# GRU stage: ScalarE writes the conditioning shift into the accumulation banks, fewer fill products, one VectorE operation for the early part of the state

## The reference, cut to what matters

```
h = 0
for t in range(128):
    z = sigmoid(x[t] @ Wz + h @ Uz + cond @ Cz + bz)
    r = sigmoid(x[t] @ Wr + h @ Ur + cond @ Cr + br)
    cand = tanh(x[t] @ W + (r * h) @ U + cond @ C + b)
    h = (1 - z) * h + z * cand
    out[t] = h
```

## Time and profile before

| | |
|---|---|
| time, median of 3 runs | 4519.89 us (4518.96 to 4525.05) |
| profiled execution, own time | 4519.17 us |
| span of its instructions | 4517.4 us, mean granted TensorE clock 0.969 |
| TensorE busy, whole span | 4151.1 us, 92% |
| VectorE busy | 2454.7 us, 54% |
| ScalarE busy | 1958.4 us, 43% |
| GpSimd busy | 782.6 us, 17% |

### The profile page before, as it was taken

The page is one execution under the profiler, slowest core; times in us unless marked ns, Lnnn a source line. Parts: engine busy times, 40 slices in busy tenths (PEclk is TensorE's granted clock), DMA queues, the critical chain, the costliest instruction groups (busy, mean ns, idle before and its releaser), DMA issues. The chain is left out here.

```text
span 4517.4 us, 116966 instructions
## 1 busy us (share of the span) xinstructions
PE 4151.1 (92%) x40700; PEld 2927.5 (65%) x40896; DVE 2454.7 (54%) x7214; ACT 1958.4 (43%) x4989; POOL 782.6 (17%) x3252
## 2 busy tenths in 40 slices
PE   6998999999998899998799998999998797889999
PEld 4555776778776455554355787887876455556666
DVE  5775664555554677775555344666666553431111
ACT  4333443333332666665233222666665352333333
POOL 1111221000000466664222000111111210000000
PEclk9999999999999999999799998999999898989999
DMA  1000000000000000000000000000000100000000
GB/s 55 0 0 25 1 0 26 1 0 0 0 0 10 1 2 1 1 1 1 34 0 0 4 0 0 3 3 3 3 3 2 54 0 1 0 0 3 5 5 7
DMA packets 4098, 29.01 MB, mean 6 GB/s; under 512 B 433, under 2 KB 945, under 8 KB 2353
## 3 DMA queue, kind: packets, MB, share of 16 engines
q1 hardware_dynamic: 3776, 24.97, 1.4%
HBM read 22.87 MB, written 2.10 MB: 6 GB/s over the span
## 5 line engine op out<-in xcount | busy, mean ns | idle before, releaser
L604 DVE TENSOR_REDUCE cells_row_max<-banks 128x4 f32<-128x512 f32 x384 | 238.5, 684 | 162.2 <-PE banks L397 162.2
L2619 ACT ACTIVATE experts_hidden<-banks,weights 128x512 f32<-128x512 f32 x256 | 175.8, 687 | 263.2 <-PE banks L2561 261.6
L2569 PEld LDWEIGHTS banks<-weights,experts_hidden 128*128 128x128 f32 x2048 | 238.6, 192 | 30.1 <-issue 30.1
L761 PE MATMUL banks<-clock_fill 128*128 128x512 bf16 x830 | 252.0, 389 | 6.4 <-issue 1.6
L2561 PE MATMUL banks<-act_a,weights 128*128 (+1 forms) x512 | 245.5, 610 | 11.3 <-PEq L101 10.8
L2639 DVE SCALAR_TENSOR_TENSOR experts_acc<-banks,experts_gate,experts_acc 128x128 f32<-128x128 f32 x224 | 63.1, 344 | 348.3 <-PE banks L2569 348.3
L541 ACT ACTIVATE cells_probs<-banks 128x512 f32<-128x512 f32 x384 | 198.3, 602 | 97.0 <-PE banks L437 90.0
L2569 PE MATMUL banks<-weights,experts_hidden 128*128 128x128 f32 x2048 | 238.8, 274 | 0.0
L604 DVE TENSOR_REDUCE attn_row_max<-banks 128x4 f32<-128x512 f32 x256 | 159.0, 684 | 134.6 <-PE banks L397 134.6
L2837 ACT ACTIVATE lin_context_turned<-banks 128x256 f32<-128x256 f32 x128 | 49.2, 384 | 403.7 <-PE banks L2789 403.7
L1578 ACT ACTIVATE wave_hidden_turned<-banks,weights 128x128 f32<-128x128 f32 x512 | 205.9, 455 | 15.9 <-PE banks L1522 12.7
(11 more groups left out here) (534 smaller groups left out, 10173.4 us busy)
## 6 DMA issues: line engine op xcount, KB each, us to landing
weights<-in_p SPq DMA_DIRECT2D x1, 2894.5 KB, 17.3
weights<-in_p SPq DMA_DIRECT2D x1, 2894.0 KB, 9.4
weights<-in_p SPq DMA_DIRECT2D x2, 1396.0 KB, 7.4
x_res<-in_x SPq DMA_DIRECT2D x1, 2048.0 KB, 15.1
out_x<-x_res SPq DMA_DIRECT2D x8, 256.0 KB, 2.0
weights<-in_p SPq DMA_DIRECT2D x1, 1836.0 KB, 10.9
weights<-in_p SPq DMA_DIRECT2D x1, 1835.5 KB, 6.9
weights<-in_p SPq DMA_DIRECT2D x1, 1344.5 KB, 9.8
```

The costliest lines, as they stand in the source:

```text
L604: dve.tensor_reduce(mt[:, 4 * g:4 * g + 4], bank, AX_X, ALU.max).then_inc(s["max_ready"], 1)
L761: pe.matmul(core.ps[:, bank, :], core.fill[:, 0:P], core.fill[:, :], start=True, stop=True)
L2569: last = pe.matmul(ps[:, OUT + e % 2, t * P:(t + 1) * P], hs[:, e % 2 * DEPTH + f, t * P:(t + 1) * P], w("W2", (e * DEPTH + f) * P, P), st ...
L2619: act.activation(hs[:, e % 2 * DEPTH + f, :], ps[:, f % 2, :], ACT.Gelu, bias=w("b1", j, 1)).then_inc(s["h_ready"], 1)
```

## The change

- The identity product of `pre` goes. ScalarE instead copies the broadcast shift into a bank (128x128 float32) once its last reader, an operation of ScalarE, is done: R at position 3, Z at position 0, CAND at position 1 of a group, always between z and cand. TensorE's x product adds onto it after a wait on `shift_set`. The banks are seeded once ahead of the loop by six identity products, where three stood.
- Fills: none at positions 0 to 2 while `pre` runs, two in the middle of the other steps, none at a step's end. Before there were two in steps at positions 0 to 2 and four at position 3.
- `zh` and `rest` become one operation, `less = (z - 1) * h`. `ahead` multiplies it by negated copies of `Ur` and `Uz`, made ahead of the loop, and the state is zc - less.
- A loop function `run` replaces `time_loop`, and passes the group's number for the wait on `shift_set`.

```diff
+        def run(eng, step):
+            for k in range(UNROLL_T):
+                step(k, k, k // AHEAD)
+            with eng.Fori(0, P // UNROLL_T - 2) as i:
+                for k in range(UNROLL_T):
+                    step(i * UNROLL_T + (UNROLL_T + k), k, i * 2 + (2 + k // AHEAD))
...
+            def seed(which, parity):
+                pe.matmul(group_bank(which, parity), const("ident"), shifts(which), start=True, stop=False,
+                          skip_group_check=True)
+
             def pre(base, parity, which):
-                bank, x_w = ((R, "Wr"), (Z, "Wz"), (CAND, "W"))[which]
-                out = ps[:, bank + parity, 0:AHEAD * NB].rearrange("p (t b) -> p t b", t=AHEAD)
-                pe.matmul(out, const("ident"), shift[:, which:which + 1, :].broadcast_to([P, AHEAD, NB]), start=True,
-                          stop=False, skip_group_check=True)
-                pe.matmul(out, w(x_w), positions(core.x, base, AHEAD), start=False, stop=False,
-                          skip_group_check=True)
+                pe.matmul(group_bank(which, parity), w(("Wr", "Wz", "W")[which]), positions(core.x, base, AHEAD),
+                          start=False, stop=False, skip_group_check=True)
...
-                past(pe, rest_ready, t)
-                rec(R, "Ur", rest[:, :, :], False)
-                rec(Z, "Uz", rest[:, :, :], False)
+                past(pe, less_ready, t)
+                rec(R, negated[:, 0, :], less[:, :, :], False)
+                rec(Z, negated[:, 1, :], less[:, :, :], False)
...
-                more = not isinstance(t, int) or t < P - AHEAD
-                if k % AHEAD < 3 and more:
-                    pre(t + (AHEAD - k % AHEAD), 1 - parity, k % AHEAD)
-                fill_clock(pe, core, 1 if k % AHEAD < 3 else 3)
+                which = k % AHEAD
+                if which < 3 and (not isinstance(t, int) or t < P - AHEAD):
+                    past(pe, shift_set, g * 3 + (which - 2))
+                    pre(t + (AHEAD - which), 1 - parity, which)
+                else:
+                    fill_clock(pe, core, 2)
                 pe.wait_ge(rh_ready, t + 1)
-                rec(CAND, "U", rh[:, :, :], True).then_inc(cand_done, 1)
+                rec(CAND, w("U"), rh[:, :, :], True).then_inc(cand_done, 1)
                 if not isinstance(t, int) or t < P - 1:
                     ahead(t + 1, k + 1)
-                fill_clock(pe, core, 1)
...
             for which in range(3):
+                for parity in range(2):
+                    seed(which, parity)
                 pre(0, 0, which)
             fill_clock(pe, core, FIRST_FILLS)
+            pe.wait_ge(negated_ready, 2)
...
+            def set_shift(which, parity):
+                act.activation(group_bank(which, parity), shifts(which), ACT.Copy).then_inc(shift_set, 1)
+
...
+                if k % AHEAD == 3 and more:
+                    act.wait_ge(r_ready, t + 1)
+                    set_shift(0, bank)
+                if k % AHEAD == 0 and more and not (isinstance(t, int) and t == 0):
+                    act.wait_ge(z_ready, t)
+                    set_shift(1, 1 - bank)
+                if k % AHEAD == 1 and more and not (isinstance(t, int) and t == 1):
+                    act.wait_ge(cand_ready, t - 1)
+                    set_shift(2, 1 - bank)
...
+            for i, name in enumerate(("Ur", "Uz")):
+                dve.tensor_scalar(negated[:, i, :], w(name), -1.0, None, ALU.mult).then_inc(negated_ready, 1)
...
-                dve.tensor_tensor(zh[:, :, :], z[:, :, :], state(t), ALU.mult).then_inc(zh_ready, 1)
-                dve.wait_ge(zh_ready, t + 1)
-                dve.tensor_tensor(rest[:, :, :], state(t), zh[:, :, :], ALU.subtract).then_inc(rest_ready, 1)
+                dve.scalar_tensor_tensor(out=less[:, :, :], in0=z[:, :, :], scalar=1.0, in1=state(t),
+                                         op0=ALU.subtract, op1=ALU.mult).then_inc(less_ready, 1)
...
-                dve.tensor_tensor(positions(core.a, t), zc[:, :, :], rest[:, :, :], ALU.add).then_inc(h_ready, 1)
+                dve.tensor_tensor(positions(core.a, t), zc[:, :, :], less[:, :, :], ALU.subtract).then_inc(h_ready, 1)
```

More of the change, by code:

```diff
@@ L1875, in gru_stage @@
         shift = sb("shift", [P, 3, NB])
[L1876 to L1880, removed]
+        r, z, rh, cand, less, zc = (sb(n, [P, 1, NB]) for n in ("r", "z", "rh", "cand", "less", "zc"))
+        negated = sb("negated", [P, 2, P])
+        (r_done, z_done, cand_done, r_ready, z_ready, rh_ready, cand_ready, less_ready, zc_ready, h_ready,
+         zeroed, cond_done, shift_ready, negated_ready, shift_set) = map(sem, [
+             "r_done", "z_done", "cand_done", "r_ready", "z_ready", "rh_ready", "cand_ready", "less_ready",
+             "zc_ready", "h_ready", "zeroed", "cond_done", "shift_ready", "negated_ready", "shift_set"])
         block = ctx.enter_context(nc.Block())
@@ L1886, in state, with group_bank, shifts @@
             return start_state[:, :, :] if isinstance(t, int) and t == 0 else positions(core.a, t - 1)
+        def run(eng, step):
[4 more added lines that the diff above has]
+                    step(i * UNROLL_T + (UNROLL_T + k), k, i * 2 + (2 + k // AHEAD))
+            for k in range(UNROLL_T):
+                t = P - UNROLL_T + k
+                step(t, k, t // AHEAD)
+        def group_bank(which, parity):
+            bank = (R, Z, CAND)[which] + parity
+            return ps[:, bank, 0:AHEAD * NB].rearrange("p (t b) -> p t b", t=AHEAD)
+        def shifts(which):
+            return shift[:, which:which + 1, :].broadcast_to([P, AHEAD, NB])
         @block.sync
@@ L1915, in rec @@
                 def rec(bank, weight, moving, stop):
-                    return pe.matmul(ps[:, bank + parity, lo:lo + NB].unsqueeze(1), w(weight), moving, start=False,
+                    return pe.matmul(ps[:, bank + parity, lo:lo + NB].unsqueeze(1), weight, moving, start=False,
                                      stop=stop, skip_group_check=True)
@@ L1923, in ahead, with step @@
                 _, rec = recurrent(k)
-                past(pe, rest_ready, t)
-                rec(R, "Ur", rest[:, :, :], False)
-                rec(Z, "Uz", rest[:, :, :], False)
-            def step(t, k):
+                past(pe, less_ready, t)
+                rec(R, negated[:, 0, :], less[:, :, :], False)
+                rec(Z, negated[:, 1, :], less[:, :, :], False)
+            def step(t, k, g):
                 parity, rec = recurrent(k)
                 past(pe, zc_ready, t)
-                rec(R, "Ur", zc[:, :, :], True).then_inc(r_done, 1)
-                rec(Z, "Uz", zc[:, :, :], True).then_inc(z_done, 1)
-                more = not isinstance(t, int) or t < P - AHEAD
-                if k % AHEAD < 3 and more:
-                    pre(t + (AHEAD - k % AHEAD), 1 - parity, k % AHEAD)
-                fill_clock(pe, core, 1 if k % AHEAD < 3 else 3)
+                rec(R, w("Ur"), zc[:, :, :], True).then_inc(r_done, 1)
+                rec(Z, w("Uz"), zc[:, :, :], True).then_inc(z_done, 1)
+                which = k % AHEAD
[4 more added lines that the diff above has]
+                    fill_clock(pe, core, 2)
@@ L1946, in _, with step @@
             fill_clock(pe, core, FIRST_FILLS)
+            pe.wait_ge(negated_ready, 2)
             ahead(0, 0)
-            time_loop(pe, step)
+            run(pe, step)
         @block.scalar
         def _(act):
-            def step(t, k):
+            def set_shift(which, parity):
+                act.activation(group_bank(which, parity), shifts(which), ACT.Copy).then_inc(shift_set, 1)
+            def step(t, k, g):
                 bank = k // AHEAD % 2
+                more = not isinstance(t, int) or t < P - UNROLL_T + 2
@@ L1958, in step @@
                 act.activation(z[:, :, :], in_group(ps[:, Z + bank, :], k), ACT.Sigmoid).then_inc(z_ready, 1)
+                if k % AHEAD == 3 and more:
[7 more added lines that the diff above has]
+                    set_shift(2, 1 - bank)
                 act.wait_ge(cand_done, t + 1)
                 act.activation(cand[:, :, :], in_group(ps[:, CAND + bank, :], k), ACT.Tanh).then_inc(cand_ready, 1)
-            time_loop(act, step)
+            run(act, step)
         @block.vector
@@ L1967, in _ @@
             dve.memset(start_state[:, :, :], 0.0).then_inc(zeroed, 1)
-            dve.memset(rest[:, :, :], 0.0).then_inc(zeroed, 1)
+            dve.memset(less[:, :, :], 0.0).then_inc(zeroed, 1)
             dve.memset(zc[:, :, :], 0.0).then_inc(zeroed, 1)
+            for i, name in enumerate(("Ur", "Uz")):
+                dve.tensor_scalar(negated[:, i, :], w(name), -1.0, None, ALU.mult).then_inc(negated_ready, 1)
             dve.wait_ge(zeroed, 3)
```

4 lines of the change are left out of this document (2 added, 2 removed).

## The result

The changed kernel takes **4577.12 us** (median of 4 runs, 4574.18 to 4580.88), the kernel before 4521.14 us on the same chip (4 runs, 4518.96 to 4525.05): ratio 1.0123 [1.0110, 1.0136]. It is slower, as predicted; 4585 was forecast, 8 us too much. The profiled execution took 4574.18 us around a span of 4572.4, 55.0 more than before.

A forecast was written before the change was run, and what follows sets the result against it. The dependent chain plus TensorE's queue was taken to bound GRU steps. At half clock the loop adds 62.5 us, last step 0.7, seeds 0.6, next stage 1.8: +65.6, giving 4585 us, range 4545 to 4600 (8 in 10).

The forecast's parts named there:

- The chain of 1.86 us: GRU step: dependent chain alone takes 0.23 + 0.71 + 0.23 + 0.69 = 1.86 us; the rest is TensorE's queue.
- The gain at full clock, 35.6 us: GRU stage if TensorE kept its clock: 39.8 us saved, less 3.6 for loop turns and 0.6 for seeds.
- rival (a): GRU stage: the clock stays full, so the kernel gets faster, 4484 us; chance 0.10.
- The step that decides, the clock: GRU stage: without the wide work the clock falls within the first few steps and stays at 1.2 GHz; chance 0.80.
- Rival (b): GRU stage: the clock falls but returns for part of the stage; +15 us, 4535 at half the time each; chance 0.08.
- The long step at half clock, 2.56: GRU steps with `pre`: 12 passes at 0.214 us take 2.56 us, TensorE's queue being the bound.
- The short step, 2.99: GRU steps without `pre` at half clock: 10 passes and 2 fills, 2.14 + 0.85 = 2.99 us.
- The loop turn: VectorE's late loop turn in 14 GRU steps: 0.26 us each, 3.6 us, counted in the full-clock sum.
- The edges: Around the GRU loop: seeds +0.6 us, last step 0.7 more, next stage's first 20 passes at half clock +1.8.
- (c): ScalarE in the GRU stage: each copy makes it load a table twice, 238 us on top, over 4750; chance 0.02.
- (d): ScalarE copies of 0.46 us delay cand: 1 us at full clock, nothing at half; no separate chance given.

The follow-up runs named there:

- the last version: The changed kernel plus a 256-column product in steps with `pre`, a whole fill ending every step and a 128-column product ending positions 0 to 2; 4488.65 us, ratio 0.9932.
- e7_merge_alone: The kernel before with only zh and rest merged into less, with negated weights; identity product and fills as before; 4522.08 us, ratio 0.9996.
- e4_narrow_fills: The changed kernel with two 32-column bf16 products added behind the x product in steps with `pre`; 4605.08 us, ratio 1.0183.

## Why the prediction was right, by its steps

**What bounded the kernel before.** Right. The chain of 1.86 us shows itself in the two steps before the fall (1.84, 1.89) and in the short steps of the last version. One reading was off: a pass was put at 0.13 us at full clock, from four weight loads in 0.52. That time includes the whole of the last load. In the kernel before the four passes on rest start at 2605.29 and the fill behind them at 2605.74, which is 0.11 a pass. Nothing hung on it, as twelve passes stay below the chain either way.

**The gain at full clock, 35.6 us.** The mechanism is shown: taking the identity and the fills out of the way is worth up to that, and rival (a)'s 4484 us is where the best executions with half fills came out (4483.34 to 4489). By its parts it is a little less: 242.3 us for the 127 steps of the last version, where the prediction's terms give 276.0 - 39.8 + 3.6 = 239.8. Long steps are 1.90 and not 1.86 there, and a loop turn costs 0.21 and not 0.26. And the gain is not there for the change as written. With fills that hold the clock 23 us of it were left in the middle of the step, and 29 when most of them stood at its end.

**The step that decides, the clock.** Right in all of it: the fall within the first few steps (the second, 3.5 us behind the first reset gate), no return for the rest of the stage, though every fourth step has two fills. Rival (b), a return for part of the time, did not come. What was argued from other stages' rows is now shown in this one by a pair: the change with the old fills keeps 1.00, the old kernel with the new fills falls to 0.50.

**The long step at half clock, 2.56.** Measured 2.56, and TensorE's queue is what sets it, at the pace of its weight loads: they start 0.20 to 0.22 us apart through the whole step, so twelve times 0.214 is right. The products themselves start less evenly. From x's first pass to the first on rh are 0.58, from there to less 0.27; together 0.85, four times 0.214.

**The short step, 2.99.** Too long: 2.83. That is the term that was mis-sized: 34 x 0.16 = 5.4 us. A fill takes 0.42 (0.427 was counted), but the weights for the product behind it load beneath it (0.76 us of weight load from 2601.76, while the second fill streams), and the two passes on rh then take 0.28 and not 0.43. Adding the price of each product as if it stood alone counts that load twice. The sum itself has a small slip beside it: 93 x 2.56 + 34 x 2.99 is 339.7 and not 340.1.

**The loop turn.** It was put at nothing for half clock. Steps at the turn take 2.65, as rh starts 0.43 after r and TensorE gets it too late: 14 x 0.09 = 1.3 us that the sum lacked. The two steps at full clock saved 1.4 us and not 1.6. With these the stage comes to 339.7 - 5.4 + 1.3 - 1.4 = 334.2, measured 334.1.

**The edges.** The seeds were put at +0.6 and seem to have taken nothing: from the stage's first instruction (ScalarE's table load) to the first reset gate are 13.17 us, against 13.30 before. But the granted clock also rises in this stretch, under the fills, and not at the same point in each profiled execution. Executions that are alike in this show the price (us from the stage's first instruction):

| version | clock rises to 1.00 | first reset gate |
|---|---|---|
| e7_merge_alone, three seeds | 6.33 | 12.47 |
| the changed kernel, six seeds | 6.43 | 13.17 |
| the kernel before, three seeds | 8.00 | 13.30 |
| e4_narrow_fills, six seeds | 8.07 | 13.98 |

That is 0.70 and 0.68 for the seeds, close to the forecast. The changed kernel's profiled execution had the luck of an earlier rise.

The last step's end came 0.5 us later (0.7 forecast), 2.28 us from the last r to the end of h against 1.75. The next stage does start at 0.50. Its first product with the cells' keys (line 397) shows the price, in the kernel before and in the changed one:

```profile
2819.94 0.81 PE L397 MATMUL banks<-cells_k_masked,cells_query 32*128 32x256 f32 x4 [1.00 <-ACT cells_query L3098]
```

```profile
2875.47 0.81 PE L397 MATMUL banks<-cells_k_masked,cells_query 32*128 32x256 f32 x4 [0.95 <-ACT cells_query L3135]
```

The end of h was at 2792.58 and 2846.81, so 27.37 us became 28.66: +1.3, where +1.8 was forecast. The term set 20 passes' busy time of 2.48 us against 4.3, but they took 2.8 with the gaps between them.

Predicted +65.6 on the span, measured +55.0. Of the 10.6 between, 5.1 lie in terms of the change that were too large: 4.4 in the stage's 127 steps, 0.2 in the last step and 0.5 in the next stage. The other 5.5 are scatter between executions: the clock's rise 0.7, the stage's earlier start 4.3, and 0.5 less behind that product of line 397.

**Copies, merge, tables.** Copies of 0.276 us (0.27 taken) and 0.212 for less (0.25 was the far end), both hidden; one table load of 1.28 us in the stage. Rivals (c) and (d) did not come. The merge alone measured as no change.

## What to carry to other kernels

Products that only keep TensorE's clock are part of the schedule: before any are taken out, look at the granted clock of stages with the same mix of wide and narrow products, and price the rest of the stage at 0.50. If the fills are in the way, move them to where the engine waits for its last input (they cost nothing there at full clock) rather than drop them, and run the result many times, since a mix at the edge gives 4483 in one execution and 4620 in the next. A fill that doesn't hold the clock should go altogether; it is the dearest choice of the three.

## What the runs showed of the hardware that was not expected

- Between no fills and enough of them, more made it slower. In shares of each version's own before: none 1.0094, two in short steps 1.0123, one more in each long step 1.0219. Faster were only versions with more of them, the fills of before (0.9946) and those of the last version (0.9932).
- The same binary kept or lost the clock from one execution to the next (13 executions, 4483.34 to 4619.95 us).
- A pass that follows a 512-column product costs 0.07 us instead of 0.214 at half clock (the pair on rh 0.28 instead of 0.43), since its weights load beneath it. Elsewhere the weight loads set the pace, one every 0.20 to 0.22 us at half clock, ahead of 32 columns as ahead of 128.
- ScalarE wrote 128x128 float32 from SBUF into a bank in 276 ns, about as fast as its copy of that size out of a bank (269).
- Where the clock rises under the fills ahead of the loop differs between profiled executions (6.33 to 8.07 us into the stage in the four of the table above), and is worth 0.8 us there.
